# A transformer layer on eight cores: the second x tile waits for the values' first weights, two value projections and a gate product change places on TensorE

## The reference

```
x = x + attention(layernorm(x))         # 32 heads of 64, 8 key/value heads, biases bq bk bv bo
x = x + ffn(layernorm(x))
ffn(h) = (silu(h @ Wg.T) * (h @ Wu.T)) @ Wd.T     # 8192 hidden
Wg = (gate_w - 128) * gate_scale[:, None]          # int32 in 0..255; Wu and Wd alike
```

## Time and profile before

| | us |
|---|---|
| median of 3 runs | 2027.4 (2023.74 to 2028.51) |
| the profiled execution, its own time | 2026.54 |
| its span, slowest core (core 1) | 2025.0 |
| the fastest core (core 2) | 2020.3 |
| PE busy | 1975.2 (98%) |
| DVE busy | 1038.9 (51%) |
| ACT busy | 1059.9 (52%) |

### The profile page before, as it was taken

One profiled execution on the slowest core, in us unless ns is written; L12 is line 12 of the kernel. 1 busy time (PEld: TensorE's weight loads), 2 busy tenths in 40 slices (PEclk: granted clock), 3 DMA queues, 4 the chain that ended last, 5 costly groups with the idle time before them and its releaser, 6 DMA issues.

```text
span 2025.0 us, 31971 instructions; the slowest of 8 cores (2020.3 to 2025.0 us)
## 1 busy us (share of the span) xinstructions
PE 1975.2 (98%) x11664; PEld 985.2 (49%) x11664; DVE 1038.9 (51%) x1425; ACT 1059.9 (52%) x1203; POOL 124.8 (6%) x177
## 2 busy tenths in 40 slices
PE   5999999999999999999999999999999999999999
PEld 3545555555555554444444444444444444444444
DVE  5624666666666667666666666666666102020202
ACT  2425889888888854544454444444544233223230
POOL 2000110110001100000000000000000000000000
PEclk9999999999999999999999999999999999999999
DMA  9628644442138348555555445544445857474651
GB/s 231 192 42 141 98 70 74 74 86 46 32 64 129 88 134 197 111 105 110 113 111 105 84 86 93 93 84 84 86 90 94 214 122 150 79 151 83 123 123 42
DMA packets 47382, 214.24 MB, mean 106 GB/s; under 512 B 5888, under 2 KB 5888, under 8 KB 30080
## 3 DMA queue, kind: packets, MB, share of 16 engines
q0 software_dynamic: 20160, 134.23, 38.8%
q1 hardware_dynamic: 27072, 77.98, 12.9%
HBM read 319.14 MB, written 27.26 MB: 171 GB/s over the span
## 4 chain that ended last, share of the span: by engine, by line
PE 93%; DMA 3%; DVE 2%; issue 1%; ACT 1%; DVEq 0%; ACTq 0%; POOLq 0%; SPq 0%
PE PS_B L166 22%; PE PS_D L166 20%; PE PS_C L166 20%; PE PS_A L166 19%; PE PS_D L162 4%; PE PS_B L162 3%; PE PS_C L162 2%; PE PS_A L162 2%; DMA arena<-wq 2%; DVE arena L200 1%; DMA arena<-wv 1%; PE PS_D L177 1%; DVE bns L200 1%; DVE arena L202 1%; DMA arena<-xt 0%
## 5 line engine op out<-in xcount | busy, mean ns | idle before, releaser
L166 PE MATMUL PS_D<-arena 128*128 128x256 bf16 (+1 forms) x2674 | 527.8, 320 | 14.3 <-DVE arena L200 11.2
L187 ACT ACTIVATE arena<-arena 128x1024 bf16<-128x1024 bf16 x384 | 379.9, 1048 | 289.2 <-DMA arena<-dwt 289.2
L166 PE MATMUL PS_B<-arena 128*128 128x512 bf16 (+1 forms) x2413 | 516.6, 357 | 0.2 <-DVE arena L200 0.2
L166 PE MATMUL PS_A<-arena 128*128 128x512 bf16 (+2 forms) x2175 | 458.8, 355 | 10.5 <-DMA arena<-wv 7.7
L166 PE MATMUL PS_C<-arena 128*128 128x512 bf16 (+1 forms) x2200 | 467.7, 354 | 0.8 <-ACT arena L187 0.8
L166 PEld LDWEIGHTS PS_B<-arena 128*128 128x128 bf16 (+1 forms) x2413 | 211.9, 97 | 259.7 <-issue 34.5
L187 ACT ACTIVATE arena<-PS_B 128x1024 bf16<-128x1024 f32 (+1 forms) x203 | 194.3, 957 | 265.8 <-PE PS_B L162 265.6
L166 PEld LDWEIGHTS PS_D<-arena 128*128 128x128 bf16 x2674 | 239.8, 98 | 177.0 <-issue 79.0
L200 DVE TENSOR_TENSOR arena<-arena 128x1024 bf16<-128x1024 bf16 (+2 forms) x500 | 301.8, 622 | 11.8 <-ACT arena L187 2.7
L200 DVE TENSOR_TENSOR arena<-PS_A,arena 128x512 f32<-128x512 f32 (+1 forms) x106 | 74.1, 699 | 455.0 <-PE PS_A L162 455.0
L166 PEld LDWEIGHTS PS_C<-arena 128*128 128x128 bf16 (+1 forms) x2200 | 190.8, 97 | 234.8 <-issue 34.3
(11 more groups left out here) (45 smaller groups left out, 893.7 us busy)
## 6 DMA issues: line engine op xcount, KB each, us to landing
arena<-gwt POOLq DMA_DIRECT2D x32, 1024.0 KB, 9.0
arena<-uwt POOLq DMA_DIRECT2D x32, 1024.0 KB, 9.0
arena<-dwt POOLq DMA_DIRECT2D x32, 1024.0 KB, 9.8
arena<-xt SPq DMA_DIRECT2D x16, 1024.0 KB, 13.3
arena<-wq POOLq DMA_DIRECT2D x32, 512.0 KB, 7.6
arena<-wo POOLq DMA_DIRECT2D x6, 2048.0 KB, 24.6
arena<-xt SPq DMA_DIRECT2D x32, 256.0 KB, 7.1
x2d<-arena SPq DMA_DIRECT2D x32, 256.0 KB, 6.5
```

Of the source, the lines that this page charges most:

```text
L166: e.matmul(o, ll, rr, start=a, stop=b, skip_group_check=k))
L187: e.activation(o, i, f, bias=b, scale=s)
```

## The change

1. SP waits for WV0 before the load of x tile 1 and no longer behind it.
2. The two biases are issued behind x tile 2 and no longer behind tile 3.
3. On PE the values of tiles 1 and 2 stand in front of the transposes of tiles 2 and 3. From tile 3 on the order is as before: step 3 has the transposes of tile 4, then the values of tile 3.
4. Product 4 of unit 0 is split: its first six matmuls stay in front of the transposes of tile 7, its last two go behind them, in front of product 5.

```diff
@@ def ld_x(g)
-            if g == 3:
+            if g == 2:
                 y_dma("XDC", bvbb[:], bvb[:])
                 xd_consts[1] = y_dma("XDC", bk2b[:], bk2[:])
@@
         ld_x(0)
+        y_wait("WV0", wd_wv[0])
         ld_x(1)
-        y_wait("WV0", wd_wv[0])
         ld_x(2)
         ld_x(3)
@@
         for g in range(16):
+            if 1 <= g <= 2:
+                vproj(g)
             if g + 1 < 16:
                 tr1(g + 1)
                 trev(g + 1)
-            if g:
+            if g > 2:
                 vproj(g)
@@
-        def product(u, j, bank, first, last):
+        def product(u, j, bank, first, last, cs=range(8)):
             w = wop(u, j)
             if u == 0 and j in dve_xs:
                 t_wait(DVE, dve_xs[j])
-            for c in range(8):
+            for c in cs:
                 mm(BK(bank), w[c], xops[j][c], start=(first and c == 0),
                    stop=(c == 7), inc=(c == 7), skip=not first)
@@ gu_unit, u == 0
-                product(0, 4, bd, True, False)
+                product(0, 4, bd, True, False, range(6))
                 norm7()
+                product(0, 4, bd, True, False, range(6, 8))
```

## The result

The changed kernel took 2036.43 us in the median of 9 runs, the kernel before 2026.95 us beside it. Three of the nine runs fell in a slower state of the chip and stay out of the ratio; the other six have a median of 2033.9 us. So the change costs 5.7 to 7.3 us by the two ratios, and their intervals reach from 3.6 to 9.9. The profiled execution took 2037.14 us with a span of 2035.6 us on core 7, where the other cores took 2023.9 to 2028.4.

The account below looks back on a forecast made before the run. PE, busy 98%, was taken as the bound, so only its idle stretches and clock could move the time. Order and load 2.7, clock 1.7 and split 0.4 gave +4.8 us on 2026.5: 2031.3, shown median 2032, range 2026.5 to 2037.

Parts of the forecast that it names:

- Within 0.3%: Whole kernel: time stays within 0.3% of the kernel before, about 6.1 us; chance 0.68.
- The load: Start: WV0 lands at 13.8, tile 1 at 24.9, 5.2 us later; tile 2's statistics at 29.9, DVE's row 1.3 us later.
- The order: PE at the start: later copies and new waits of 1.8 and 1.4 us put tile 4's values at 52.5, +2.7 us.
- The clock: Tile 1's values: PE idles 3.5 us and resumes at the low clock; +1.7 us, ends 0 and 2.9.
- The reference core: Start measured by core 1, where tile 4's values began at 49.76; claimed +4.4 us there.
- The split: Around tile 7's transposes: product 5 starts 0.1 to 0.65 us later; taken as +0.4, upper end another 1.5.
- Rival 1: Start: tile 1 lands early at 22.7, clock high, almost no loss, about 2028.3 us; chance 0.16.
- rival 3: PE at the start: tile 1's values move into idle time and it gains, at best 2026 us; chance 0.08.
- Rival 2: Start: tile 1 lands at 28.5, +8.4 us, 2035.8; or tile 2's wait keeps the clock low, 3.4 more; chance 0.22.

Follow-up runs that it names:

- e1: Kernel before with only the x tile 1 load behind WV0 and the biases behind tile 2; ratio 1.0016 to before, mean of the cores +1.4 us.
- e6: Changed kernel with ACT's copies of tile 1 in front of the two activations for tile 2; ratio 1.0019 to before, mean of the cores +3.5 us.
- e5: The changed kernel run again, the second comparison; ratio 1.0028 to the kernel before, mean of the cores +5.6 us.
- e7: Changed kernel with seven unread filler matmuls in the wait in front of tile 1's values; ratio 1.0027 to before, mean of the cores +3.4 us.
- e3: Kernel before with only the split of product 4; ratio 1.0008 to before, mean of the cores +0.7 us.
- e12: Changed kernel with the first two output projection weight loads issued later, in the attention; ratio 1.0008 to before, mean of the cores +2.8 us.
- e8: Kernel before, its loads kept, with tile 1's transposes, copies and values moved earlier; ratio 1.0006 to before, mean of the cores +0.4 us.
- e2: Kernel before with only the values of tiles 1 and 2 in front of the transposes of tiles 2 and 3; ratio 1.0021 to before.
- e10: Kernel before with product 4 of unit 0 computed twice in a row; ratio 0.9993 to before, mean of the cores -0.7 us.
- e11: Kernel before with e9's late loads and e10's doubled product; ratio 0.9971 to before, mean of the cores -4.1 us.
- e4: Changed kernel without the split of product 4; ratio 1.0047 to before, mean of the cores +4.9 us.
- e9: Kernel before with the first two output projection weight loads issued 32 and 64 steps later in the attention; ratio 0.9979 to before.

## Why the prediction was right, and what was mis-sized

The mechanism came out step by step. The direction held and the forecast of +4.8 us was low: 5.6 on the mean and 5.7 to 7.3 on the slowest core. The median of 2036.4 lies just under the upper end of the range, 2037, and that of the six other runs, 2033.9, well inside it. "Within 0.3%", which I gave 0.68, held in the second comparison (0.28%) and not in the first (0.36%), whose interval covers both; the data do not tell the two apart.

- **The load.** Forecast landing 24.9 and tile 2's statistics 29.9; tile 1's statistics started at 24.4 to 26.1 and tile 2's at 30.0 on the mean. WV0 was there at 15.95 on core 7 (15.5 to 16.1 over the cores) and not at 13.8 (8.5 + 5.0 is 13.5; for the 0.3 more I gave no reason), and tile 1 took 8.6 to 9.95 us and not 11.05. The two errors have opposite signs and met within half a microsecond, which is luck. e1 prices the load alone at +1.4.
- **The order.** Forecast 35.35 for tile 1's values (35.5 measured), 1.8 us in front of tile 2's (1.73), 1.4 around tile 4's transposes (0.82 + 0.31 = 1.13). Right within 0.3 us. e6 confirms the role of ACT's order.
- **The clock.** Taken at 1.7, with ends 0 and 2.9. The 15 steps took 5.08 us on the mean of the first profile (5.39 in e5) for 3.24 at the high level, so 1.8 (2.1), and e7 gives 2.1. This is the one term in the start that was too small. I also misread where it shows: I wrote that the granted clock reads 1.00 throughout, which holds for core 1 before, but not for the cores that lost: core 0 before reads 0.83 from 20 to 30 us and again to 40. The Trainium skill (TensorE: Matmul & The Clock Gate, Part 4: PE-mode transpose) denies that transposes count for the clock. No run was made to tell, but the rows lean against it. The low stretch in tile 1's values is twice what their 15 steps exceed 3.24 us. Behind 3.28 us of idle (32 cores) it lasted 2.6 to 5.9 us; where transposes ran straight into the products (39 cores that were low there, in the kernels with the old order) it lasted 1.1 to 4.3, and under 2.6 on 20 of them.
- **The reference core.** I measured the start by core 1 (49.76) while the mean of the cores was 49.5, and core 1 got off lightly after (53.4, mean 54.6). Core by core the shift was +3.6 to +6.6, mean 5.2, against my 4.4; the means over all profiles, 50.1 and 55.3, give 5.2 too.
- **The split.** Forecast +0.4, from +0.1 at the high clock to +0.65 at the low one. Measured at tile 7: 0.0 and +0.2, with the clock +0.3; on the whole kernel +0.7 in e3, standard error 0.26. The sign was right and the size is not contradicted, but it rests mostly on how often the clock is low there, which is open (last section).
- **The slowest core.** Not in my sum at all, and the term that was missing. The first comparison's extra came in part from the wait for the queries' weights, which I saw in the rows as 2.5 us and did not ask about on other cores. It is not made by the change: 19 of 528 spans stand out in the kernel before, 3 of 48 in the changed one at first and 2 of 80 in e5, and e12 shows the same cost with the wait removed. That the change lets it grow longer where it does strike is neither shown nor excluded.

Rival 1 is out (tile 1 never landed before 24.3), rival 3 too: e8 shows that even with copies in time nothing is gained, as DVE's row holds PE. Rival 2 put the time 8.4 us above before; 5.7 to 7.3 came, and by neither of its two ways. Tile 1 landed at 24.3 to 26.0 and not at 28.5, and the new wait in front of tile 2's values did not keep the clock low: behind 1.73 us of idle these matmuls took 3.40 us, the high level, on all 56 cores of the seven kernels that have the new order.

## What to carry to other kernels

Work that moves forward on an in-order engine costs time unless its own input is ready, and even then it gains only if nothing else holds the engine later (e8); ask which cover its producer loses, and what stands in front of that producer on its own engine (here two tiny activations were worth 2 us). Price an idle stretch of TensorE together with the matmuls behind it. And before shaving waits at the start, look at all cores for the wait that decides which one is slowest: moving two early loads out of the way gave 4.2 us on the slowest core and 2.8 on the mean, where this change took 5.7 and 5.6.

## What the runs showed of the hardware

- The clock fell in an idle of a few microseconds here and came back late. After 2.2 to 4.4 us of idle the products of all cores in e2, the changed kernel and e5 ran at 1.2 GHz for a while, 15 steps in 4.6 to 6.2 us. Stretches of core 1 of the changed kernel, then of core 3 of e7; the third number from the end is the granted clock:

```profile
30.00:36.00 6.00, 2.72 (x18) 1.65 (x17) 5.11 (x9) 2.33 (x4) 3.09 (x4) 0.50 1.00 344
36.00:42.00 6.00, 4.61 (x30) 2.34 (x28) 5.60 (x11) 2.24 (x4) 0.00 (x0) 0.87 1.03 221
```

```profile
30.00:36.00 6.00, 4.36 (x24) 2.65 (x25) 5.11 (x9) 2.33 (x4) 2.05 (x2) 0.64 0.98 320
36.00:42.00 6.00, 4.42 (x32) 2.35 (x31) 5.70 (x10) 2.43 (x4) 1.09 (x3) 1.00 1.03 249
```

  With the filler the clock is up (1.00) from 36 us on, when tile 1's values run; without it they run at 0.50 for the greater part. In the first 20 us the record says 1.00 although the first transposes (7 in 0.91 us, where 0.55 is the high level) are slow, so there only the spacing shows the level.
- A wait of 1.73 us left the clock up on 56 of 56 cores in front of tile 2's values. At tile 7, 0.50 us of idle left the clock up on 16 of 16 cores (e10, e11). With 2.23 us it was down on 27 of 48 cores (before, e1, e2, e4, e8, e9), with 2.66 us on 34 of 48 (after, e3, e5, e6, e7, e12). So the added 0.43 us may make it likelier, but the counts of single kernels run from 2 to 8 of 8 at the same idle; what decides between them is open.
- With no load of x beside it the weights' load did not reach the rate of the long average. WV0 took 14.0 to 14.6 us from its issue, where my 168 GB/s from 8.5 us on had given 12.3. From 8.5 to 16 us the engines of core 7 were full (share 0.99) at 146 GB/s, the last number here:

```profile
8.50:16.00 7.50, 1.87 (x16) 1.63 (x16) 4.09 (x6) 1.35 (x3) 1.18 (x1) 1.00 0.99 146
```

  These are 1.10 MB, and I had counted 0.84 for the rest of WV0; the other 0.26 MB are probably the head of WV1, the next load in that queue, but no run shows whose they are.
